# Retention in a fused two-branch block: keys spread by VectorE out of PSUM, and the retention reordered on four engines

## What is computed

```python
xn = channel_group_norm(x, norm_g, norm_b, H)            # H = 16 heads of 8 channels
q = l2_normalize(xn @ qw.T)
k = l2_normalize(xn @ kw.T)
v = xn @ vw.T
sim = jnp.einsum('bhnd,bhmd->bhnm', qh, kh) * scale
sim = sim * dmask[None]                                  # gamma ** (n - m), causal
yh = jnp.einsum('bhnm,bhmd->bhnd', sim, vh)
y = y @ ow.T + ob
```

## Time and profile before

| | |
|---|---|
| median of 3 runs | 961.44 us (960.83 to 963.38) |
| the profiled execution | 963.04 us |
| its span, first to last instruction | 961.0 us |
| mean granted TensorE clock, as a share of full speed | 0.985 |

### The profile page before, as it was taken

The page is one execution under the profiler, slowest core; times in us unless marked ns, Lnnn a source line. Parts: engine busy times, 40 slices in busy tenths (PEclk is TensorE's granted clock), DMA queues, the critical chain, the costliest instruction groups (busy, mean ns, idle before and its releaser), DMA issues.

```text
span 961.0 us, 26494 instructions
## 1 busy us (share of the span) xinstructions
PE 867.1 (90%) x10900; PEld 586.1 (61%) x10900; DVE 633.6 (66%) x1082; ACT 559.5 (58%) x1105; POOL 631.0 (66%) x500
## 2 busy tenths in 40 slices
PE   0678899989999899998998989999999999999986
PEld 0346565766667656666576655666666666666652
DVE  5875676756857667576676775858586767676732
ACT  0336575566656667566575647575757566666551
POOL 4588587675866767767767564858585858575701
PEclk9979999999999999999999999999999999999998
DMA  9211210211202112011121121213131313121000
GB/s 297 47 26 23 40 41 16 46 22 34 47 16 45 23 30 49 17 39 28 21 54 19 31 48 23 56 29 72 29 74 27 75 26 75 33 66 38 25 23 11
DMA packets 127873, 41.80 MB, mean 44 GB/s; under 512 B 103778, under 2 KB 126988, under 8 KB 127628
## 3 DMA queue, kind: packets, MB, share of 16 engines
q1 hardware_dynamic: 122500, 38.82, 18.0%
q10 hardware_dynamic: 5256, 1.31, 0.7%
HBM read 9.70 MB, written 2.10 MB: 12 GB/s over the span
## 4 chain that ended last, share of the span: by engine, by line
PE 61%; DVE 16%; POOL 10%; ACT 6%; issue 5%; DMA 1%; DVEq 0%; POOLq 0%; SPq 0%; ACTq 0%
PE pQK L1208 9%; PE pT L1119 5%; PE pV L1173 5%; PE pT L1076 5%; PE pS L1108 4%; DVE m L757 4%; PE pS L1135 4%; PE pM L1285 4%; PE pM L1152 4%; PE pT L1268 3%; PE pQK L1376 3%; POOL rn L422 3%; DVE ss L770 2%; POOL m L435 2%; POOL qkn L442 2%
## 5 line engine op out<-in xcount | busy, mean ns | idle before, releaser
L422 POOL TENSOR_TENSOR rn<-rn,half_neg 128x16 f32<-128x16 f32 x64 | 187.5, 2930 | 5.3
L435 POOL TENSOR_TENSOR m<-m 128x1024 f32<-128x1024 f32 x64 | 150.9, 2357 | 0.0
L420 POOL TENSOR_SCALAR rn<-ss 128x16 f32<-128x16 f32 x64 | 16.3, 255 | 187.9 <-DVE ss L770 186.7
L1208 PE MATMUL pQK<-wqkv,hT 128*128 128x512 f32 x256 | 125.0, 611 | 4.9 <-DVE m L757 4.9
L442 POOL TENSOR_TENSOR qkn<-m,rn 128x1024 f32<-128x1024 f32 x64 | 121.7, 1902 | 5.0
L805 DVE TENSOR_REDUCE mx<-pS 128x8 f32<-128x1024 f32 x64 | 78.1, 1220 | 63.8 <-PE pS L1108 63.7
L580 ACT ACTIVATE prT<-pT 128x1024 f32<-128x1024 f32 x64 | 65.6, 1025 | 70.7 <-PE pT L1119 70.5
L596 ACT ACTIVATE sq<-pQK 128x1024 f32<-128x1024 f32 x64 | 65.5, 1023 | 35.1 <-PE pQK L1208 35.0
L770 DVE TENSOR_REDUCE ss<-sq 128x16 f32<-128x1024 f32 x64 | 77.6, 1212 | 7.1 <-ACT sq L596 6.9
L564 ACT ACTIVATE kT<-pT 128x512 f32<-128x512 f32 x64 | 38.3, 598 | 73.7 <-PE pT L1076 73.7
L807 DVE TENSOR_TENSOR pr<-pS,mx 128x1024 f32<-128x1024 f32 x64 | 78.4, 1225 | 2.2
(11 more groups left out here) (164 smaller groups left out, 1876.5 us busy)
## 6 DMA issues: line engine op xcount, KB each, us to landing
vmix<-vown SPq DMA_DIRECT2D x124, 128.0 KB, 2.7
kT<-kT SPq DMA_DIRECT2D x60, 128.0 KB, 2.7
x<-in_L_attn_x SPq DMA_DIRECT2D x4, 512.0 KB, 9.7
hT<-xnT SPq DMA_DIRECT2D x64, 32.0 KB, 1.9
xs<-in_L_attn_x SPq DMA_DIRECT2D x8, 256.0 KB, 3.2
hT<-x2T SPq DMA_DIRECT2D x64, 32.0 KB, 1.9
out<-aqkT SPq DMA_DIRECT2D x8, 256.0 KB, 2.2
wqkv<-in_L_ffn_wqkv SPq DMA_DIRECT2D x2, 768.0 KB, 10.0
```

Of the source, the lines that this page charges most:

```text
L422: eng.tensor_tensor(rn[:, k % 2, :], rn[:, k % 2, :], half_neg[:, 0:2 * H], ALU.pow).then_inc(S["rn_done"], 1)
L435: eng.tensor_tensor(m1[:, k % 2, :], m1[:, k % 2, :], m2[:, :], ALU.add).then_inc(S["add_done"], 1)
L1208: mm = eng.matmul(pQK[:, g * 512:(g + 1) * 512], hT[:, k, :], wqkv[:, l, g * 512:(g + 1) * 512], start=True, stop=True)
```

## The change

Five things are done, all in the retention of layer 0 and in slots 2 and 3 around it:

1. `kx` is no longer made by GpSimd out of `aqkT`. VectorE makes it, out of PSUM (`dve_place_keys`). ScalarE's copy shrinks from 128x256 (queries and keys) to 128x128 (queries).
2. GpSimd does the first retention norm ahead of the scaling of attention batch 2, which moves from slot 2 to slot 3. Then it places the queries of batch 0, and only then norms batch 1.
3. TensorE transposes retention batch 0 in slot 3, ahead of the attention's weighted values, into pT instead of pM (`turned_bank`). `qx` of batch 0 lies in `prT`, which those weighted values read, so GpSimd's first `qx` waits for `o_mm`.
4. The bodies of `pe_retention`, `act_retention` and `dve_retention` are written out batch by batch in a new order. On TensorE the scores of a batch come ahead of its sums, and the transposes of the next batch behind them; the last transposes of `xr` wait for `kx` of batch 3.
5. On VectorE the output `o` of attention batch 0 moves behind both halves of the rotation and behind `aqk` of batch 1; the sum of squares moves into the retention. On ScalarE the exponential of batch 1 moves further back.

```diff
+        def turned_bank(b):
+            return pM if b else pT
...
+            if k == 2 and new and new[0] == 0:
+                pool_norm(eng, count(new, k), k)
+                pool_add(eng, count(new, k), k)
+                return
             if retain:
                 pool_retention_norm(eng, new[1], 0)
+                pool_scale(eng, count(new, 2), 2)
                 return
...
+            pool_place_queries(eng, t, 0)
             pool_retention_norm(eng, t, 1)
-            for b in range(NB):
-                pool_mask_qk(eng, t, b)
-                if b + 2 < NB:
-                    pool_retention_norm(eng, t, b + 2)
+            pool_retention_norm(eng, t, 2)
+            pool_place_queries(eng, t, 1)
+            pool_retention_norm(eng, t, 3)
+            pool_place_queries(eng, t, 2)
+            pool_place_queries(eng, t, 3)
...
+            if b == 0:
+                eng.wait_ge(LS["o_mm"], count((0, t), 0) + 1)
...
+            eng.activation(aqkT[:, b % 2, 0, :], turned_bank(b)[:, 0:P], ACT.Copy).then_inc(A["t_ev"], 1)
...
+            act_retention_queries(eng, t, 0)
+            act_retention_values(eng, t, 1)
+            act_retention_squares(eng, t, 2)
+            act_place_values(eng, t, 0)
+            act_retention_queries(eng, t, 1)
+            act_retention_values(eng, t, 2)
+            act_exp(eng, 1, count((0, t), 1))
+            act_retention_squares(eng, t, 3)
+            act_place_values(eng, t, 1)
+            act_retention_queries(eng, t, 2)
+            act_retention_values(eng, t, 3)
+            act_place_values(eng, t, 2)
+            act_retention_queries(eng, t, 3)
+            act_place_values(eng, t, 3)
...
+        def dve_place_keys(eng, t, b):
+            n = 4 * t + b
+            shape = [P, NBL, NG, BL]
+            eng.wait_ge(A["t_ev"], n + 1)
+            need(eng, A["st_mm"], n - 1)
+            eng.tensor_tensor(kx[:, b % 2, :, :, :],
+                              turned_bank(b)[:, P:2 * P].rearrange("p (c n) -> p c n", c=NBL).unsqueeze(2).broadcast_to(shape),
+                              place_mask.unsqueeze(1).unsqueeze(3).broadcast_to(shape), ALU.mult).then_inc(A["kx"], 1)
...
+            if k == NB - 1 and new and new[0] == 0:
+                pe_retention_turn(eng, new[1], 0)
...
+            if old:
+                eng.wait_ge(A["kx"], 4 * t + 4)
+                pe_ln(eng, old)
```

More of the change, by code:

```diff
@@ L586, in act_slot @@
             if k == NB - 1 and new and new[0] == 0:
-                act_retention_project(eng, new[1], 0)
+                act_retention_squares(eng, new[1], 0)
+                act_retention_values(eng, new[1], 0)
             if k == 0 and turned:
@@ L608, in act_slot @@
             if k == NB - 1 and new and new[0] == 0:
-                act_retention_project(eng, new[1], 1)
+                act_retention_squares(eng, new[1], 1)
             else:
@@ L908, in dve_retention_qk, with dve_block_sums @@
                                          op1=ALU.mult).then_inc(A["qk"], 1)
+        def dve_place_keys(eng, t, b):
+            n = 4 * t + b
+            shape = [P, NBL, NG, BL]
[4 more added lines that the diff above has]
+                              place_mask.unsqueeze(1).unsqueeze(3).broadcast_to(shape), ALU.mult).then_inc(A["kx"], 1)
+        def dve_block_sums(eng, t, b):
+            eng.wait_ge(A["kv_mm"], 4 * t + b + 1)
+            need(eng, A["state"], t)
+            eng.tensor_tensor(before[:, b, :, :], pS[:, 0:P].rearrange("p (c n) -> p c n", c=NBL),
+                              same_head, ALU.mult).then_inc(A["kvm"], 1)
         def dve_retention(eng, t, old):
+            dve_block_sums(eng, t, 0)
             eng.wait_ge(LS["qkn_done"], 4 * t + 3)
[L912 to L924 removed]
+            dve_block_scores(eng, t, 0)
+            dve_place_keys(eng, t, 1)
+            dve_retention_qk(eng, t, 2)
+            dve_block_sums(eng, t, 1)
+            dve_block_scores(eng, t, 1)
+            dve_place_keys(eng, t, 2)
+            dve_retention_qk(eng, t, 3)
+            dve_sum_squares(eng, count((0, t), NB - 1), NB - 1)
+            dve_block_sums(eng, t, 2)
+            dve_block_scores(eng, t, 2)
+            dve_place_keys(eng, t, 3)
+            if old:
+                dve_ln(eng, old)
+            dve_block_sums(eng, t, 3)
+            dve_block_scores(eng, t, 3)
         def dve_block_scores(eng, t, b):
@@ new lines, in pe_retention @@
+            pe_retention_project(eng, t, 2)
+            eng.wait_ge(A["kx"], 4 * t + 1)
+            pe_block_values(eng, t, 0)
+            pe_block_scores(eng, t, 0)
+            pe_block_sums(eng, t, 0)
+            pe_retention_turn(eng, t, 1)
+            pe_retention_project(eng, t, 3)
+            pe_block_output(eng, t, 0)
+            pe_block_scores(eng, t, 1)
+            pe_block_values(eng, t, 1)
+            pe_block_sums(eng, t, 1)
+            pe_retention_turn(eng, t, 2)
+            pe_block_output(eng, t, 1)
@@ L1324, in pe_block_values @@
+            pe_block_scores(eng, t, 2)
+            pe_block_values(eng, t, 2)
+            pe_block_sums(eng, t, 2)
+            pe_retention_turn(eng, t, 3)
+            pe_block_output(eng, t, 2)
+            if old:
+                eng.wait_ge(A["kx"], 4 * t + 4)
+                pe_ln(eng, old)
+            pe_block_values(eng, t, 3)
+            pe_block_sums(eng, t, 3)
+            pe_block_scores(eng, t, 3)
+            pe_block_output(eng, t, 3)
         def pe_block_values(eng, t, b):
```

89 lines of the change are left out of this document (26 added, 63 removed).

## The result

The changed kernel takes 970.76 us against 962.06 us for the kernel before (medians of 8 runs each, interleaved): ratio 1.0088, 95% interval 1.0072 to 1.0104. One execution of the eight (1150.79 us at a granted clock of 0.754) is left out of the ratio, and without it the median is 969.67. Timed again among the experiments it took 966.90 us, ratio 1.0068 (1.0046 to 1.0091). It is slower by 0.7 to 0.9%; the prediction was 965.0, with 968.5 as its upper end.

What follows compares the result with a forecast made beforehand. TensorE, busy 90% of the span, was taken as the bound. Seven steps by 0.67 (4.7), 0.2 for the first and minus 1.2 for gaps gave plus 3.7 on 961.44, rounded 965.0 us; range 959.5 to 968.5.

Steps and rivals of the forecast that it cites:

- The waits: TensorE in the retention: about 1 us for `o`, 1.0 for `qx` of batch 2, half a us for keys before `xr`.
- the 0.4 for `vx`: Retention batch 2: TensorE waits some 0.4 us for `vx`, the values of batch 1 that ScalarE places.
- The two unmeasured durations: ScalarE's 128x128 copy, taken as 0.28 us from 0.20 to 0.39; VectorE's keys, taken as 0.69 from 0.69 to 1.04.
- The turn starts 0.22 behind the sums: Retention batch 1 on TensorE: the turn starts at 508.43, 0.22 us behind the sums, and ends 0.41 later.
- the forecast's 0.67: Clean later layer-0 step: 0.67 us slower, ending at 521.99 against 521.32; seven steps make 4.7 us.
- The first step, priced at 0.2: First layer-0 step, without `xr` or an old step beside it: the same placement gives it 0.2 us.
- The gaps: Short unexplained gaps late in the retention, 2.4 us over seven steps; half disappear into the new waits, minus 1.2 us.
- so for the median it is 961.44 plus 3.7: Profiled execution lay 1.6 us above the median of the runs, so plus 3.7 on 961.44 gives 965.0 us, rounded.
- Slower by more: Rival, chance 0.10: keys at 1.04 and copies at 0.39 in each step, no gap hidden, 9.7 us more, 971.1.
- No change: Rival, chance 0.33: gaps vanish wholly (minus 2.4) and copies cost 0.20, so plus 0.8 us, 962.2.
- The faster case: Rival: waits for `xr`, `o` and mask go, 2.12 us a step, 944.5; chance of over 0.3% faster 0.12.
- three parts in four of 0.45: Share of the forecast case (963.6 to 967.5, chance 0.45) counted as slower: 0.36 of the 0.50 for slower.

Runs made afterwards that it cites:

- the run with ScalarE's copy first: Changed kernel with turns 2 and 3 directly behind the scores and ScalarE copying queries ahead of placing values: 961.89 us, ratio 1.0015 to the kernel before.
- keys alone: Kernel before with only the keys moved: VectorE spreads them out of PSUM, ScalarE copies queries only: 978.49 us, ratio 1.0166.
- keys on GpSimd: Changed kernel with its keys given back to GpSimd, out of a 128x256 copy: 991.48 us, ratio 1.0325 to the kernel before.
- norm late: Changed kernel with GpSimd's scaling of batch 2 back ahead of the first retention norm: 980.85 us, ratio 1.0210 to the kernel before.

## Why the prediction missed

*The waits, right in place and size.* Moved to the start of the profiled step (502.64 for 502.16, 0.48 later), the forecast had the first sums at 508.69; they started at 508.71. It said about 1 us for `o` (1.09), about 1 for the queries of batch 2 (0.92, behind the chain through the placing, as the run with ScalarE's copy first confirms), and half a us for the transposes of `xr` (0.47). Only the 0.4 for `vx` was nearly nothing.

*The two unmeasured durations, right.* Rows of the changed kernel, ScalarE's copy and VectorE's keys:

```profile
503.95 0.28 ACT L671 ACTIVATE aqkT<-pT 128x128 f32<-128x128 f32 x1
...
504.59 0.68 DVE L938 TENSOR_TENSOR hidden<-pT,cst 128x512 f32<-128x512 f32 x1
```

0.28 was taken for the copy and 0.69 for the keys. The estimate of 0.25 for the copy from "VectorE: DVE Perf Modes" of the Trainium skill, section on the TRN2 errata, lies 0.03 under the row.

*The step that failed: "The turn starts 0.22 behind the sums".* That was the distance from sums to the first part of the output, of one narrow matmul to the next; I used it for a narrow one followed by a full one. It is 0.35 to 0.38. The same slip stands at more places: scores to values 1.06 for 0.98 in two batches, the transposes of `xr` 0.98 for 0.91, and the last scores 0.38 behind the sums for 0.22. Against the shifted forecast TensorE is 0.15 late at turn 1, 0.21 at the scores of batch 1, 0.34 at those of batch 2, 0.40 at `xr`, and 0.62 at the last scores (520.67 for 520.05) and the next step. Of the 0.62, these passages make 0.5 and the handoffs between engines 0.1; no wait is longer than forecast by more than 0.1. One more, output behind turn 0.37, I had wrong too, but it costs nothing, since TensorE waits for the queries behind it. The mechanism forecast (the chain of batches 1 to 3 through placing, copy and spread) was right, and its terms were too small: the forecast's 0.67 became 1.3, which over seven steps is 4.3 us. The first step, priced at 0.2, took 0.8 longer from its last attention projection on.

*The gaps.* I let half of 2.4 us vanish; all did: the six later steps of the changed kernel's profile lie between 62.28 and 62.33. That gave back 1.2. The Trainium skill, "Runtime: NRT & Kernel Launch", section Instruction fetch mechanics, calls the crossing of a 16 KiB block mostly hidden; that these gaps are instruction fetches no run here shows.

*From one execution to the median: the second step that failed.* The words "so for the median it is 961.44 plus 3.7" took the changed kernel's median to lie 1.6 us below its profiled execution, as it did for the kernel before. It lay 4.7 above it (970.76 against 966.08; 3.6 with 969.67). In numbers this is the whole miss: for the profiled execution the sum said 966.7 and 966.08 was measured. That agreement is luck, since the longer steps were paid for by 3.7 us from the first window and the second step, both at a higher granted clock than before. The medians differ by 8.7 us in the first timing and 5.4 in the second. Over the 13 other runs of both timings the median of the changed kernel is 967.6, inside the range; the first timing, with its four runs at 0.983 and less, is not. No execution at 0.979 was profiled, so where its 5 us go is open, and so is why the changed kernel had such runs. I had left the run's clock out of the range.

*The rivals.* "Slower by more" gave 971.1, near the number, for the wrong reason: keys and copies cost what I had taken. "No change" had the vanished gaps right. The faster case fell on ScalarE's placing, as predicted: "by the rows they take 3.1" us against TensorE's 1.6. One slip in the chances: three parts in four of 0.45 are 0.34 and not 0.36, so "slower" should have had 0.48.

*By parts, in clean steps.* Norm first: −0.9 (on the order of before) and −1.45 (in the changed order). Keys on VectorE on top of it: +1.3. The reordering on top of both: +0.9 (61.4 to 62.29). The three add up to the measured +1.3, as they must, each being the difference from one kernel to the next.

## What to carry to other kernels

Price a reordering by the distance between the very two operations that will be neighbours, kind to kind: here a turn between sums and output costs TensorE 0.30 us more than one beside the scores (2.08 against 1.78). Then ask if anything waits there: moving the turns back made the step 0.45 longer, and only the order of ScalarE's list gave the time back. When an operation is moved to an engine with slack, look at what stands behind it there, and price the queue: the same keys cost 1.3 us on VectorE in one order and saved 2.4 in another. And try the parts alone: a change of five parts that lost 0.7 to 0.9% held one that gains 0.7% in five lines.

## What the hardware showed that I had not expected

- Neighbours of another kind cost TensorE time. Sums to output 0.22 us, sums to turn 0.35 to 0.38; turn to scores 0.28 to 0.33, turn to values 0.31, turn to output 0.37; scores to turn 0.97, scores to values 0.98 to 1.06. The runs show the sizes, not the mechanism, and not that such passages make up all of the 1.1 us by which TensorE is busier in a step.
- The granted clock fell inside layer-0 steps in two kernels (keys alone, keys on GpSimd), after stretches in which TensorE worked about half the time. Steps of 62.5 to 63.0 became 63.9 to 64.8 in the first, and steps of 64.7 became 65.3 to 66.6 in the second. Like stretches went by at 1.00 in the same executions (392 to 396 above). With waits of 1.26 and 1.01 us, but apart, it stayed at 1.00 (norm late).
- "issue" need not mean issue: in the kernel with the keys on GpSimd the same wait of the scores appears as 2.0 us for GpSimd's `prT` in some steps and as 2.02 us for issue in others. What the short gaps of the earlier trace rows are therefore stays open.
